# Attention and feed-forward block on one core: two pair blocks and their normalizations at earlier places of a hand-written order

## The reference

```python
qkv = x @ w_qkv.T + b_qkv                  # 16 heads of 32
scores = q @ k.T / sqrt(32)                # causal
out = softmax(scores) @ v
x = layernorm(x + out @ w_out.T + b_out)
hidden = relu((x @ sign(up_w).T) * up_scale)
x = layernorm(x + (hidden @ sign(down_w).T) * down_scale * output_scale)
```

## Time and profile before

| | us |
|---|---|
| median of 3 runs | 773.69 |
| lowest, highest run | 773.59, 777.36 |
| profiled execution, its own time | 774.34 |
| span of its trace | 772.6 |
| TensorE busy in the span | 722.7 (94%) |
| VectorE, GpSimd, ScalarE busy | 450.5, 354.4, 317.2 |

### The profile page before, as it was taken

How to read it: one execution, slowest core, us unless ns; L and a number is a source line. 1 busy time by engine, 2 the same in 40 slices (tenths; PEclk the granted TensorE clock), 3 DMA queues, 4 the chain that set the end, 5 groups by cost and what they waited for, 6 DMA issues and landing times.

```text
span 772.6 us, 11683 instructions
## 1 busy us (share of the span) xinstructions
PE 722.7 (94%) x4032; PEld 505.2 (65%) x4032; DVE 450.5 (58%) x1086; ACT 317.2 (41%) x631; POOL 354.4 (46%) x487
## 2 busy tenths in 40 slices
PE   6899999999999999999979889999999999999993
PEld 4788665655656556565544544788778787878882
DVE  4176495785967859678567751633294339334515
ACT  5211365654655546555546565432232222122210
POOL 4461467394673946739423502632353235223333
PEclk9999999999999999999999999999999999999998
DMA  6976464435544355452677331313012001000101
GB/s 231 296 208 177 110 174 124 136 105 163 150 132 132 108 157 148 115 133 88 174 206 261 109 123 58 120 32 119 14 41 95 28 1 41 15 1 12 44 1 54
DMA packets 44619, 85.71 MB, mean 111 GB/s; under 512 B 4880, under 2 KB 13584, under 8 KB 44432
## 3 DMA queue, kind: packets, MB, share of 16 engines
q1 hardware_dynamic: 35536, 79.72, 34.2%
q10 hardware_dynamic: 9024, 5.24, 2.4%
HBM read 55.33 MB, written 29.36 MB: 110 GB/s over the span
## 4 chain that ended last, share of the span: by engine, by line
PE 71%; DVE 19%; issue 3%; DMA 3%; POOL 2%; ACT 2%; SPq 0%; ACTq 0%; POOLq 0%
PE ps_heads L1045 9%; PE ps_proj L1087 7%; DVE heads_sb L835 7%; PE ps_proj L947 7%; PE ps_score L1104 6%; PE ps_unit L1063 6%; PE ps_unit L1087 5%; PE ps_sum L1039 5%; DVE maxes L813 5%; PE ps_unit L983 4%; PE ps_heads L1104 3%; PE ps_unit L1015 3%; PE ps_sum L1104 3%; PE ps_score L1015 2%; PE ps_score L983 2%
## 5 line engine op out<-in xcount | busy, mean ns | idle before, releaser
L655 POOL TENSOR_TENSOR hid_low<-hid_raw,hid_high 128x512 fp32r<-128x512 f32 x64 | 85.1, 1330 | 175.0 <-DVE hid_high L886 171.9
L711 ACT ACTIVATE probs<-ps_unit 128x512 f32<-128x512 f32 (+3 forms) x216 | 101.9, 490 | 88.4 <-PE ps_unit L1015 85.0
L619 POOL TENSOR_SCALAR_AFFINE_SELECT probs<-probs 128x128 f32<-128x128 f32 x256 | 73.1, 298 | 113.0 <-ACT probs L711 108.9
L711 ACT ACTIVATE probs<-ps_score 128x512 f32<-128x512 f32 (+3 forms) x155 | 75.2, 498 | 77.0 <-PE ps_score L1015 75.6
L886 DVE CAST hid_high<-hid_raw 128x512 fp32r<-128x512 f32 x64 | 27.1, 424 | 125.4 <-ACT hid_raw L766 125.2
L809 DVE CUSTOM_DVE_ANT_0 ps_unit<-ps_unit,causal 128x512 f32<-128x512 f32 (+3 forms) x162 | 80.1, 511 | 32.5 <-PE ps_unit L983 31.5
L1045 PE MATMUL ps_heads<-probs,v_rows 128*32 128x512 f32 (+3 forms) x768 | 80.3, 502 | 11.8 <-DVE heads_sb L837 11.8
L983 PE MATMUL ps_unit<-stack 96*128 96x512 f32 (+3 forms) x246 | 83.8, 354 | 5.7 <-DVE maxes L809 2.5
L1015 PE MATMUL ps_unit<-stack 98*128 98x512 f32 (+2 forms) x216 | 78.4, 366 | 4.1 <-DVE maxes L809 4.0
L613 POOL TENSOR_TENSOR parts<-qk_full,parts 128x512 fp32r<-128x512 f32 x32 | 41.3, 1289 | 64.7 <-ACT parts L690 64.4
L835 DVE RECIPROCAL heads_sb<-ps_sum 128x128 f32<-128x128 f32 x64 | 60.8, 950 | 9.2 <-PE ps_sum L1039 9.2
(11 more groups left out here) (195 smaller groups left out, 1478.0 us busy)
## 6 DMA issues: line engine op xcount, KB each, us to landing
stack<-qk_parts SPq DMA_DIRECT2D x96, 256.0 KB, 4.6
qk_parts<-parts SPq DMA_DIRECT2D x32, 512.0 KB, 2.9
v_all<-h_even ACTq DMA_DIRECT2D x16, 256.0 KB, 3.8
v_rows<-v_all SPq DMA_DIRECT2D x8, 512.0 KB, 4.3
heads_t<-heads_sb SPq DMA_DIRECT2D x16, 256.0 KB, 3.4
raw<-up_w SPq DMA_DIRECT2D x8, 512.0 KB, 3.9
x_tile<-x_rows SPq DMA_DIRECT2D x16, 256.0 KB, 5.5
raw<-down_w SPq DMA_DIRECT2D x8, 512.0 KB, 3.4
```

The source lines that it names most:

```text
L655: nc.gpsimd.tensor_tensor(hid[1][:, (HM * s + n) % 3, :], hid_raw[:, n % 2, :], hid[0][:, (HM * s + n) % 3, :].bitcast(FP32), ALU.subtract ...
L711: nc.scalar.activation(probs[:, (NP * s + n) % RING, 0:width], bank(what, s, n)[:, off:off + width], ACT.Exp, scale=SCALE).then_inc(s_exp, 1)
```

## The change

Only the tables of places are edited; no instruction is added or taken away.

```diff
-PAIRED = [13, 13, 19.6, 19.6, 28, 28, 36, 36, 44, 44, 52, 52]
-PAIRED_NORM = [19.7, 19.71, 19.72, 19.73, 52.05, 52.06, 52.07, 52.08]
+PAIRED = [13, 13, 17.8, 17.8, 28, 28, 36, 36, 44, 44, 49.6, 49.6]
+PAIRED_NORM = [17.9, 17.91, 17.92, 17.93, 49.7, 49.71, 49.72, 49.73]
...
-MAXIMA = ([11.5 + 0.5 * u for u in range(3)] + [13.4 + 0.48 * u for u in range(13)]
+MAXIMA = ([11.5 + 0.5 * u for u in range(3)] + [13.4 + 0.35 * u for u in range(13)]
...
-BLOCK = [(1, 2, 0.5, 0.98, 13.05, 15.8, 18.5), (1, 3, 13.3, 0.5, 19.65, 22.4, 24.8),
-         (2, 0, 20.5, 1.2, 34.4, 37.2, 40), (2, 1, 36.3, 0.6, 44.05, 46.8, 49.2)]
+BLOCK = [(1, 2, 0.5, 0.98, 13.05, 15.8, 18.5), (1, 3, 13.3, 0.36, 17.85, 20.6, 23),
+         (2, 0, 18.5, 1.38, 34.4, 37.2, 40), (2, 1, 36.3, 0.6, 44.05, 46.8, 49.2)]
```

## The result

The changed kernel takes 809.92 us (median of 4 runs, 808.68 to 811.84) against 774.14 us (773.59 to 777.36): a ratio of 1.0455, with a 95% interval of 1.0418 to 1.0493. It is slower by 35.8 us. The forecast was 798 us, +24.7; the time lies 0.1 us inside the upper end of its range, 810 us, where the rival stood in which the clock drops in the shift's stops too, with a chance of 0.08. The profiled execution took 811.84 us, with a span of 810.1.

The account below looks back on a forecast made before the run. TensorE, busy 94% of the span, was taken to bound the kernel. Terms 6.4 + 14.5 - 1.2 - 1.0 + 6.0 = +24.7 us on 774.34 gave 799.0, predicted as 798 us for the median; range 785 to 810.

Parts of the forecast that it names:

- the clock drops in the shift's stops too: Rival: the clock also falls in half 1's six stops for the shift, 12 us more, 810 us; chance 0.08.
- What bounds, and what could be won: TensorE, busy 94% of the span, bounds; its 13 waits for norms before value products total 11.8 us.
- The rival for faster: VectorE serves the copy and shift_l in idle time ahead of the norms: 9.3 us won, 764 us; chance 0.03.
- The copy: Half 0, steps 0, 2, 4: w_high behind four norms delays the pair at 28 by 4.82 us each, +14.5 us.
- 14.5 - 1.2 - 1.0 + 6.0: Copy stops +14.5, earlier norms in odd steps -1.2, step 6 -1.0, clock loss behind three copies +6.0 us.
- The shift: Half 1, steps 1 to 6: shift_l behind four norms holds a bank the fifth score needs; +1.06 each, +6.4 us.
- The clock in the shift's stops: Half 1's six stops for the shift were taken to leave the granted clock up: 0 us.
- the pause of 2.23 us: TensorE's pause ahead of the steps in the profile before, after which the clock stayed at 1.00.
- The bound of 2.0 each: Upper end for clock loss in half 1's six shift stops: 6 x 2.0 us, within the clock term's 18.0.
- The clock behind the copy: After each of half 0's three copy stops the clock falls, costing 2.0 us each, +6.0 us.
- Step 6: The 3.96 us wait for a bank goes, but a value product then waits for norms; -1 us, between 0 and -2.
- SyncE's and GpSimd's lists at nothing: Later shift transfers, store, w_low and probability sums on SyncE and GpSimd were counted as costing 0 us.

Follow-up runs that it names:

- half 0 alone: Changed kernel with half 1's pair and norms put back at 52 and 52.05: 794.62 us against 775.94, ratio 1.0253.
- experiment 1: Changed kernel with the weight copy w_high at 17.7, ahead of the four norms at 17.9: 785.87 us against 775.03, ratio 1.0136.
- experiment 6: Kernel before with only the shift of half 1 moved from 51.9 to 52.1, behind the norms: 798.96 us against 775.94, ratio 1.0312.
- Half 1 alone: Kernel before with only half 1's pair moved to 49.6 and its norms to 49.7: 791.33 us against 775.03, ratio 1.02.
- experiment 3: Changed kernel with the copy at 17.7 and the shift at 49.55, both ahead of the norms: 770.60 us against 775.03, ratio 0.9922.
- experiment 7: Kernel before with half 1's pair at 49.6, three norms from 49.7, the fourth at 51.95 behind the shift: 775.46 us against 775.94, ratio 0.9998.
- experiments 5 to 7: Half 0 alone, experiment 6 and experiment 7, at 794.62, 798.96 and 775.46 us, each timed beside the kernel before at 775.94 us.

## Why the prediction was right and where it was wrong

- **What bounds, and what could be won:** right. With the two pieces put ahead of the norms the waits of the earlier trace rows shrink as meant. The rival for faster priced this at 764 us; the version that does it ran at 770.6. Its pair at 13 still waits 0.5 us and more, which the price left at a few tenths; that is about 1 us in all. Most of the rest goes with the granted clock: two of its six runs have the mean clock that the profile before has, 0.991, and they took 766.0 us.
- **The copy:** right in place and size. Stop of 5.21 us against "some 5", and 18.7 us for half 0 alone against 14.5 - 1.2 - 1.0 + 6.0 = 18.3. Taking the copy's place back takes 25 us off, where 21 were expected (experiment 1).
- **The shift:** right in place, and the stop too: the forecast moved the fifth score by 2.45 us, and it waits 2.35, what is left once the matmuls already under way have ended. One number shows it by itself (experiment 6).
- **The clock in the shift's stops:** wrong, and it is nearly the whole of the miss: 9.9 of 11.1 us. (Half 0 has 0.4 of it, and 0.8 is what the two halves alone leave open.) The step was "0 for the six shifts", taken from the pause of 2.23 us that left the clock up, as the nearest row in length. In the changed kernel all six stops, 1.88 to 2.36 us, were followed by 0.50. Half 1 alone cost 16.3 us and not 6.4, 1.65 us more in each step. One pause early in the span, among the projections of v, was not enough of a witness: in the changed kernel the same pause, 2.39 us there, was itself followed by 0.50 (last section). The bound of 2.0 each, kept as the other end, was near. That the time still lies inside the range is owed to this end, and not to the sum.
- **The clock behind the copy:** right, 2.0 forecast. The windows of after show 0.50 from within the stop to 4.8 us after it:

```profile
216.00:217.00 1.00, 0.00 (x0) 0.81 0.67 266
217.00:218.00 1.00, 0.00 (x0) 0.50 0.00 0
219.00:220.00 1.00, 1.00 (x3) 0.50 0.95 307
223.00:224.00 1.00, 1.00 (x5) 0.78 1.09 250
224.00:225.00 1.00, 1.00 (x6) 1.00 0.85 307
```

  Measured, the work from the block's first projection to the pair at 28 takes 6.82 us here (218.68 to 225.50) and 4.78 us in experiment 3 (198.72 to 203.50), so the low clock costs 2.0 us. By the Trainium skill's two spacings (TensorE: Matmul & The Clock Gate, Part 1) half of the 4.8 us between 218.68 and the rise within the window of 223 to 224 is lost, an estimate of 2.4 us; the measurement is somewhat below it. The trace agrees with the page that a busy engine that is made to stop pays again after the stop: the clock is 0.50 from 219 to 223, after TensorE has begun again.
- **Step 6:** right. The wait for a bank became one for the norms (3.58 us, the longer of the two on `heads_sb` in the waits above). With half 0 alone the first pv of half 1 there begins 17.44 us after the step's first pv, before 18.91: -1.5 us against -1.
- **SyncE's and GpSimd's lists at nothing:** none of TensorE's waits of after names the low weights of the copies, and the only one for a transfer is the pause ahead of the steps, 2.4 us, which the kernel before has too. So nothing speaks against it.

## What to carry to other kernels

When a long piece of work is moved up in an in-order engine's list, look at the short pieces it overtakes: a copy of 0.69 us and a row operation of 0.28 us were what TensorE needed next, and each became late by four norms. Pull the short pieces along and the move pays; here that turned +36 us into -4.4. And price a stop of TensorE with the clock behind it: a stop of 2.35 us cost 2.7 us a step here, after what the earlier pair won back, and 1.6 us of that were the clock's; one of 1.15 us cost only itself.

## What the runs showed of the hardware that was not expected

The granted clock is not a matter of the stop's length alone. In the profiled executions, stops of 1.15 us never lowered it (five of five in experiment 7), and those of 1.88 to 2.36 us nearly always did (all six in the changed kernel and in half 1 alone, five of six in experiment 1). But the pause ahead of the steps, which was the prediction's witness, goes either way. It left the clock at 1.00 at 2.23 us before and at 2.12 us in experiment 3, and it was followed by 0.50 at 2.39 us in the changed kernel and at 1.73 us in half 1 alone. The pause and the window behind it in the changed kernel:

```profile
35.67 0.40 PE L983 MATMUL ps_unit<-stack 96*128 96x128 f32 x1 [2.39 <-DMA stack<-qk_parts]
```

```profile
36.00:38.00 2.00, 2.00 (x7) 0.50 1.08 410
```

Shorter waits go either way too. One of 1.5 us ahead of step 0, the same in every run, left the clock at 1.00 in the changed kernel and was followed by 0.50 in experiment 3, where these rows show it:

```profile
84.69 0.70 PE L1015 MATMUL ps_score<-stack 98*128 98x512 f32 x2 [1.48 <-DVE h_even L791]
```

```profile
87.00:88.00 1.00, 1.00 (x4) 0.50 0.03 8
88.00:89.00 1.00, 1.00 (x4) 0.50 0.02 4
```

And one of 1.00 us in step 7 was followed by 0.50 in the changed kernel and not in the kernel before. So the counts above are of single executions, and a stop's length gives a likely price, not a sure one.

The times go with the mean granted clock of a run: in experiment 3 two runs took 765.94 and 765.98 us at 0.991, and four 770.05 to 771.78 us at 0.984 to 0.987. The kernel before spreads in the same way, from 772.01 us at 0.991 to 779.38 us at 0.982 beside experiments 5 to 7. What decides it for the same instructions is open; no run here separates it. In the changed kernel the clock fell 0.5 to 1.1 us after the end of a stop for the shift, and 1.8 to 2.2 us before the end of one for the copy.
